# Edges in couples of quads, with the gather's wait moved from the sums to the addition

## The reference, cut to what matters

```
h   = maximum(layernorm(x), 0)
e   = concatenate([h[src], h[dst]], axis=1)        # 200000 x 128
m   = relu(e @ W1 + b1) @ W2 + b2                  # hidden width 128, out 64
s   = segment_sum(m, dst);  cnt = segment_sum(1, dst)
out = x + s / maximum(cnt, 1)
```

## Time and profile before

| | |
|---|---|
| median of 3 runs | 2347.13 us (2336.28 to 2356.41) |
| profiled execution | 2347.96 us, its span 2346.0 us |
| mean granted clock of TensorE | 0.771 |
| busy, share of the span | PE 1445.9 us (62%), PEld 1207.9 (51%), DVE 923.2 (39%), ACT 352.7 (15%), POOL 1480.6 (63%) |
| DMA | 136.93 MB, mean 58 GB/s; the gathers' queue 17.1% of 16 engines' time |

### The profile page before, as it was taken

The page is one execution under the profiler, slowest core; times in us unless marked ns, Lnnn a source line. Parts: engine busy times, 40 slices in busy tenths (PEclk is TensorE's granted clock), DMA queues, the critical chain, the costliest instruction groups (busy, mean ns, idle before and its releaser), DMA issues.

```text
span 2346.0 us, 23165 instructions
## 1 busy us (share of the span) xinstructions
PE 1445.9 (62%) x8389; PEld 1207.9 (51%) x8390; DVE 923.2 (39%) x2278; ACT 352.7 (15%) x704; POOL 1480.6 (63%) x1572
## 2 busy tenths in 40 slices
PE   4451566666666666565666665666665656667667
PEld 3330555555555555554555554555554544555545
DVE  7240334343433343343433433443443433443434
ACT  3230111111111111111111111111111111111111
POOL 5647566666666666666666666666666666665664
PEclk8775777777777777777777778787878877887778
DMA  7532111111111111221212221221221212222221
GB/s 152 148 97 59 43 48 49 50 49 50 48 49 49 50 49 50 51 53 49 62 49 52 52 51 50 61 53 51 53 60 50 52 50 64 55 59 53 65 57 45
DMA packets 107754, 136.93 MB, mean 58 GB/s; under 512 B 30864, under 2 KB 81847, under 8 KB 107635
## 3 DMA queue, kind: packets, MB, share of 16 engines
q0 software_dynamic: 50016, 101.22, 17.1%
q1 hardware_dynamic: 57055, 33.95, 5.4%
q10 hardware_dynamic: 564, 0.23, 0.1%
HBM read 119.21 MB, written 16.07 MB: 58 GB/s over the span
## 4 chain that ended last, share of the span: by engine, by line
another core or an unknown queue 41%; PE 26%; issue 16%; DVE 14%; ACT 2%; DVEq 1%
PE bank L992 8%; PE bank L981 7%; DVE g L759 5%; DVE work L746 4%; PE bank L971 3%; PE bank L1007 2%; DVE work L739 2%; PE bank L999 2%; DVE acc L765 1%; PE bank L871 1%; ACT g L545 1%; PE bank L1017 1%; DVE raw_t L739 1%; DVE stats L612 0%
## 5 line engine op out<-in xcount | busy, mean ns | idle before, releaser
L424 POOL DMA_INDIRECT g<-p_table,src_e x1523 | 1440.9, 946 | 809.6 <-issue 422.6
L992 PE MATMUL bank<-work,g 128*128 128x128 f32 x3126 | 572.5, 329 | 119.7 <-issue 118.4
L992 PEld LDWEIGHTS bank<-work,g 128*128 128x128 f32 x3126 | 493.2, 234 | 188.2 <-issue 185.2
L545 ACT ACTIVATE g<-g 128x512 f32<-128x512 f32 x391 | 246.8, 631 | 1283.0 <-DVE g L759 1032.7
L739 DVE TENSOR_SCALAR_CACHE_REDUCE work<-bank,rows_f 128x512 f32<-128x512 f32 (+1 forms) x261 | 195.0, 747 | 482.7 <-remote 315.7
L981 PEld LDWEIGHTS bank<-work 128*128 128x128 f32 x2086 | 350.5, 238 | 23.2 <-issue 7.5
L981 PE MATMUL bank<-work 128*128 128x128 f32 x2086 | 348.9, 321 | 11.6 <-issue 11.6
L971 PE MATMUL bank<-rel_q,ident 128*128 128x512 bf16 x391 | 183.2, 468 | 254.0 <-DVE work L739 151.5
L765 DVE TENSOR_TENSOR acc<-acc,bank 65x128 f32 x199 | 55.9, 281 | 555.6 <-remote 503.1
L1007 PE MATMUL bank<-sums_u,w 128*64 128x128 f32 x398 | 104.1, 351 | 265.6 <-ACT sums_u L550 170.4
L759 DVE TENSOR_TENSOR g<-bank,g 128x512 f32<-128x512 f32 x391 | 267.7, 685 | 0.0
(11 more groups left out here) (93 smaller groups left out, 419.8 us busy)
## 6 DMA issues: line engine op xcount, KB each, us to landing
g<-p_table,src_e POOLq DMA_INDIRECT x1523
work<-q_table SPq DMA_DIRECT2D x199, 64.0 KB
p_table<-g SPq DMA_DIRECT2D x12, 448.0 KB
q_table<-work SPq DMA_DIRECT2D x12, 448.0 KB
out_dram<-xs SPq DMA_DIRECT2D x5, 448.0 KB
xs<-in_x_dram SPq DMA_DIRECT2D x2, 672.0 KB
xs<-in_x_dram SPq DMA_DIRECT2D x1, 784.0 KB
acc<-in_src_dram SPq DMA_DIRECT2D x1, 768.0 KB
```

The costliest lines, as they stand in the source:

```text
L424: nc.gpsimd.indirect_dma_start(out=g[:, slot(n), j * HID:(j + 1) * HID], out_offset=None, in_=p_table, in_offset=bass.IndirectOffsetOnAxis ...
L545: nc.scalar.activation(g[:, slot(n), 0:w], g[:, slot(n), 0:w], ACT.Relu).then_inc(r_done, 1)
L992: last = nc.tensor.matmul(u_bank[i % 2][:, 0:WIN], g[:, slot(n), HID * c:HID * (c + 1)], member[:, n % MEMBERS, c, :], start=n == GROUPS[i ...
```

## The change

The second stage goes over 196 **couples** of two quads. DVE and ACT do one operation of 1024 columns where they did two of 512, and each semaphore counts couples; in the part with one quad per group a couple holds two windows, so its spread is two operations (`PARTS`) and its two groups are one **block** with one copy and one product with W2. The broadcast on PE is gone: SP writes `rel_q` to a DRAM table once and loads four rows at a time, 4 KB each to all 128 partitions (512 KB), into two buffers, and DVE's spread reads them there. The sum of gathered and q rows no longer goes back into the ring but into one of two places of their own (`both`, a couple each); relu and `sum_edges` use it there. So the gather's wait, once per couple, is for `z_done`, DVE's addition, and the ring has 32 slots; `ahead` starts at 32 and falls by two every 24 quads, to 8. Members have two buffers of a couple and stand ahead of the addition in DVE's order. The core of the diff:

```diff
-RING = 36
-AHEAD_LEAST, AHEAD_STEP = 8, 12
+RING, SLOTS = 32, 36
+AHEAD_LEAST, AHEAD_STEP = 8, 24
 WINDOWS = 8
-MEMBERS = 4
-COUNTS = 8
+COUNTS = 16
...
+def couple(m):
+    return range(2 * m, min(2 * m + 2, QUADS))
...
+BLOCKS = []
+for i, quads in enumerate(GROUPS):
+    if quads[0] % 2:
+        BLOCKS[-1].append(i)
+    else:
+        BLOCKS.append([i])
+BLOCK = [k for m in range(COUPLES) for k, groups_k in enumerate(BLOCKS) if GROUP[2 * m] in groups_k]
+BLOCK_END = [GROUPS[groups_k[-1]][-1] // 2 for groups_k in BLOCKS]
+PARTS = [sorted({GROUP[n] for n in couple(m)}) for m in range(COUPLES)]
...
+    rel_table = nc.dram_tensor("rel_table", [QT * 128, QE], BF16).ap()
...
+        rows_of = [rel_q[:, :, :].rearrange("p t e -> p (t e)"), rows_b[:, :]]
+        g = sb("g", [128, SLOTS, 4 * HID])
         slots = g[:, :, :].rearrange("p k c -> p (k c)")
+        both = [slots[:, 512 * (RING + 2 * k):512 * (RING + 2 * k + 2)] for k in range(2)]
...
+        rows_b = sb("rows_b", [128, 4 * QE], BF16)
+        hs = rows_b[0:NP, :].bitcast(F32).rearrange("p (k t f) -> p k t f", k=HS, f=FEAT)
...
+        qw = [(work if k < 4 else w1_flat)[:, HID * (k % 4):HID * (k % 4 + 1)] for k in range(WINDOWS)]
+        member = work[:, 512:2560].rearrange("p (k c w) -> p k c w", k=2, c=8)
+        spreads = [work[:, 2560 + 1024 * k:2560 + 1024 * (k + 1)] for k in range(2)]
...
+        z_all = [ctx.enter_context(nc.psum_tensor(f"z{i}", [128, 1024], F32)) for i in range(2)]
...
+            sp.wait_ge(row_table, QT)
+            sp.dma_start(rel_table.rearrange("(t q) e -> q t e", q=128), rel_q[:, :, :]).then_inc(rel_out, 16)
...
+            def load_rows(j):
+                if j >= 2:
+                    sp.wait_ge(spread_done, parts_to(2 * (j - 1)))
+                sp.dma_start(rows_of[j % 2], rel_table[4 * j:4 * j + 4, :].rearrange("(o q) e -> o (q e)", o=1)
+                             .to_broadcast([128, 4 * QE])).then_inc(rows_there[j % 2], 16)
...
-                if n >= RING:
-                    ahead = max(AHEAD_LEAST, RING - (n - RING) // AHEAD_STEP)
-                    pool.wait_ge(u_psum, n - ahead + 1)
+                if n >= RING and n % 2 == 0:
+                    ahead = max(AHEAD_LEAST, RING - 2 * ((n - RING) // AHEAD_STEP))
+                    pool.wait_ge(z_done, (n - ahead) // 2 + 1)
                 for j in range(chunks_of(n)):
                     nc.gpsimd.indirect_dma_start(
                         out=g[:, slot(n), j * HID:(j + 1) * HID], out_offset=None, in_=p_table,
                         in_offset=bass.IndirectOffsetOnAxis(ap=src_e[:, 4 * n + j:4 * n + j + 1], axis=0))\
-                        .then_inc(gathered[slot(n)], 16)
+                        .then_inc(gathered[slot(n) // 2], 16)
...
-            def relu(n):
-                w = HID * chunks_of(n)
-                act.wait_ge(z_done, n + 1)
-                nc.scalar.activation(g[:, slot(n), 0:w], g[:, slot(n), 0:w], ACT.Relu).then_inc(r_done, 1)
-            def copy_sums(i):
-                act.wait_ge(u_psum, GROUPS[i][-1] + 1)
-                nc.scalar.copy(sums_u[:, i % 2, :], u_bank[i % 2][:, 0:WIN]).then_inc(u_copied, 1)
+            def relu(m):
+                act.wait_ge(z_done, m + 1)
+                rows = both[m % 2][:, 0:HID * chunks_in(m)]
+                nc.scalar.activation(rows, rows, ACT.Relu).then_inc(r_done, 1)
+            def copy_sums(k):
+                w = WIN * len(BLOCKS[k])
+                act.wait_ge(u_psum, BLOCK_END[k] + 1)
+                nc.scalar.copy(sums_u[:, k % 2, 0:w], u_bank[k % 2][:, 0:w]).then_inc(u_copied, 1)
...
-            def spread_of(n):
-                w = 128 * chunks_of(n)
-                dve.wait_ge(row_done, n + 1)
-                nc.vector.tensor_scalar(spreads[n % 3][:, 0:w], row_bank[:, 0:w], rows_f[:, :], 0.0,
-                                        ALU.is_equal, ALU.add, accum_out=count[:, n % COUNTS:n % COUNTS + 1])\
-                    .then_inc(spread_done, 1)
-            def members_of(n):
-                if n >= MEMBERS:
-                    dve.wait_ge(u_psum, n - MEMBERS + 1)
-                nc.vector.tensor_tensor(member[:, n % MEMBERS, :, :],
-                                        columns_p.unsqueeze(1).to_broadcast([128, 4, WIN]),
-                                        rel_e[:, 4 * n:4 * n + 4].unsqueeze(2).to_broadcast([128, 4, WIN]),
+            def spread_of(m):
+                dve.wait_ge(rows_there[m // 2 % 2], 16 * (m // 4 + 1))
+                at = 0
+                for k, i in enumerate(PARTS[m]):
+                    w = 128 * sum(chunks_of(n) for n in couple(m) if GROUP[n] == i)
+                    row = 2 * QE * (m % 2) + at
+                    j = (parts_to(m) + k) % COUNTS
+                    nc.vector.tensor_scalar(spreads[m % 2][:, at:at + w], rows_of[m // 2 % 2][:, row:row + w], rows_f[:, :],
+                                            0.0, ALU.is_equal, ALU.add, accum_out=count[:, j:j + 1]).then_inc(spread_done, 1)
+                    at += w
+            def members_of(m):
+                if m >= 2:
+                    dve.wait_ge(u_psum, m - 1)
+                nc.vector.tensor_tensor(member[:, m % 2, :, :],
+                                        columns_p.unsqueeze(1).to_broadcast([128, 8, WIN]),
+                                        rel_e[:, 8 * m:8 * m + 8].unsqueeze(2).to_broadcast([128, 8, WIN]),
                                         ALU.is_equal)
-            def add_rows(n):
-                w = HID * chunks_of(n)
-                rows_n = g[:, slot(n), 0:w]
-                dve.wait_ge(zq_done, n + 1)
-                if n < RAW:
-                    dve.wait_ge(raw_p_done, n + 1)
+            def add_rows(m):
+                dve.wait_ge(zq_done, m + 1)
+                if 2 * m < RAW:
+                    dve.wait_ge(raw_p_done, 2 * m + 2)
                 else:
-                    dve.wait_ge(gathered[slot(n)], rows_landed(n))
-                nc.vector.tensor_tensor(rows_n, z_bank[n % 3][:, 0:w], rows_n, ALU.add).then_inc(z_done, 1)
-            def add_sums(i, at):
-                v = sums[:, bass.ds(at, WIN)]
-                dve.wait_ge(v_psum, i + 1)
-                nc.vector.tensor_tensor(v, v, v_bank, ALU.add).then_inc(v_done, 1)
+                    dve.wait_ge(gathered[slot(2 * m) // 2], rows_landed(m))
+                w = HID * chunks_in(m)
+                nc.vector.tensor_tensor(both[m % 2][:, 0:w], z_all[m % 2][:, 0:w], rows_of_p(m), ALU.add)\
+                    .then_inc(z_done, 1)
+            def add_sums(k, firsts):
+                dve.wait_ge(v_psum, k + 1)
+                for j, i in enumerate(BLOCKS[k]):
+                    if j:
+                        dve.wait_ge(v_done, groups_to(k) + j)
+                    v = sums[:, bass.ds(firsts[GROUPS[i][0] % 8], WIN)]
+                    nc.vector.tensor_tensor(v, v, v_bank[:, WIN * j:WIN * (j + 1)], ALU.add).then_inc(v_done, 1)
...
-                for n in range(QUADS + 4):
-                    if n + 2 < QUADS:
-                        spread_of(n + 2)
-                    if n < QUADS:
-                        add_rows(n)
-                    if n + 1 < QUADS:
-                        if n - 1 in MEAN_AT:
-                            dve.wait_ge(o_psum, MEAN_AT.index(n - 1) + 1)
-                        members_of(n + 1)
-                    if 2 <= n < QUADS + 2:
-                        if (n - 2) % 8 == 0:
-                            firsts = first_nodes(dve, n - 2)
-                        i = GROUP[n - 2]
-                        if n - 2 == GROUPS[i][-1]:
-                            add_sums(i, firsts[GROUPS[i][0] % 8])
+                for m in range(COUPLES + 4):
+                    if m + 1 < COUPLES:
+                        spread_of(m + 1)
+                    if m < COUPLES:
+                        if m - 1 in MEAN_AT:
+                            dve.wait_ge(o_psum, MEAN_AT.index(m - 1) + 1)
+                        members_of(m)
+                        add_rows(m)
+                    if 2 <= m < COUPLES + 2:
+                        if (m - 2) % 4 == 0:
+                            firsts = first_nodes(dve, 2 * (m - 2))
+                        k = BLOCK[m - 2]
+                        if m - 2 == BLOCK_END[k]:
+                            add_sums(k, firsts)
...
-            def broadcast_rows(n):
-                w = 128 * chunks_of(n)
-                if n:
-                    pe.wait_ge(spread_done, n)
-                nc.tensor.matmul(row_bank[:, 0:w], ident16[:, n % 128:n % 128 + 1].to_broadcast([128, 128]),
-                                 rel_q[:, n // 128, 0:w], start=True, stop=True).then_inc(row_done, 1)
-            def spread_q(n):
-                pe.wait_ge(spread_done, n + 1)
-                i = GROUP[n]
-                if n == GROUPS[i][0]:
-                    pe.wait_ge(window_in[i % WINDOWS], 16 * (i // WINDOWS + 1))
-                for c in range(chunks_of(n)):
```

(77 more changed lines are left out.)

125 lines of the change are left out of this document (67 added, 58 removed).

## The result

The changed kernel takes 2539.35 us in the median (2532.87 to 2568.08), the kernel before 2344.88 beside it. The ratio is 1.084 (95% interval 1.081 to 1.088): 8.4% slower. Slower was the forecast, by 2%; the time lies outside the range, 89 us above its upper end. Of all the runs reported here one, of the kernel with half of DVE's columns, was in a slower state of the chip; the ratio leaves it out.

The account below looks back on a forecast made before the run. POOL's gather pauses, waiting for PE's late signals, were taken to bound the kernel. 2347.96 us + 52 for longer pauses + 0 for the rest = 2400, less 0.8 to the median: 2399 us; range over the cases 2250 to 2450.

Parts of the forecast that it names:

- the gather's wait, the step that decides: At POOL's gather: pause grows by 2.48 us of members and addition to 4.57, bounds 1.24 and 3.75; +52 us in all.
- What bounds the kernel: POOL's pauses at the gather, for PE's signals held up while POOL gathers: 2.09 us per 2.4 quads, 0.87 a quad.
- The round: Quads between two POOL pauses: two couples or three, 4 or 6 quads, taken as 4.5 in the mean.
- What is given back: The pipe works promptly during the longer pause: prompt stretch 9.1 instead of 6.6 us, 3.6 to 4.0 quads at its pace.
- DVE's operations, PE's relief: DVE: addition and members 1.24 us, spread 1.27, worth nothing; PE: a tenth fewer records, prompt pace 2.5 instead of 2.77 us.
- SP and DMA: 98 row loads of 512 KB cost nothing, covered by two couples; otherwise up to a few us each.
- The rows' place in SBUF: Spread reading SBUF beside POOL's gathers: nothing; bound 0.23 us for each of 196 spreads, 45 us.
- The ring: 32 places stop POOL earlier but the pipe starts some 20 us earlier too: nothing, 6 us either way.
- fewer records win: At the gather: members made before signals fail, only the addition remains, pause 3.33 us; 2301 or 2234 us, chance 0.34.
- it cancels: At the gather: 4.57 us pauses at 4.9 to 5.7 quads a round, within 23 us, 2325 to 2371; chance 0.20.
- POOL pays for the spreads: Gathers beside spreads: the spread's accumulator form holds POOL, 45 us on top, 2444; chance 0.06.
- the gate doesn't matter: At the gather: PE's recovery alone ends pauses, the addition always ready; 100 to 145 us less, 2200 to 2250; chance 0.05.

Follow-up runs that it names:

- the thirteen kernels in the table: The kernel before, the changed kernel and their follow-up variants, each with its ratio, waits and pause per quad; ratios from 0.992 to 1.110.
- couples with the old wait: The changed kernel, but its gather waits for PE's sums of the couple (`u_psum`) instead of DVE's addition: 2334.72 us, ratio 0.996.
- the twins by quads: The kernel before with four places for the sums and a ring of 32: gather waiting for DVE's addition 2494.99 us, for PE's sums 2371.88 us.
- the wait for the relu: The changed kernel, its gather waiting for ACT's relu of the couple (`r_done`) instead of DVE's addition: 2629.67 us, ratio 1.110.
- the rows alone: The kernel before, by quads, with rows brought by SP's 512 KB loads and PE's broadcast removed: 2353.92 us, ratio 0.992.
- signals per quad: The changed kernel with its gather waiting for PE's sums, `u_psum` raised and awaited per quad instead of per couple: 2386.78 us, ratio 1.008.

## Why the prediction was wrong

The mechanism and the direction were right; the step that failed is "the gather's wait, the step that decides", by the size of its term: the pause grew by 6.29 - 2.09 = 4.20 us and not by 2.48.

- *What bounds the kernel.* Held. The pauses make the difference between before and after, and the ratios of the thirteen kernels in the table follow its last column, within the first sets and within the later ones. One reading was too neat: not all of PE's signals wait until POOL is silent, as the sums addition of the earlier trace rows began at 1022.65, beside POOL's last gather.
- *The term that was mis-sized.* The pause was put at 2.09 + 2.48 = 4.57 us and is 6.29. The couples with the old wait split the missing 1.72: they have 2.86, so 0.77 come with the couples, which I had at nothing, and 6.29 - 2.86 = 3.43 with the moved wait, which I had at 2.48. The trace of the changed kernel has both parts in its 79 pauses: from the end of POOL's last gather to the first operation that DVE starts after it 3.2 us in the mean, and from there to POOL's next gather 3.5. DVE began with the members in 46 of them, and in 43 of these POOL followed 2.6 us later: there the 2.48 was right. In 27 it began with the sums addition, 3.8 us after POOL's end in the mean; POOL followed 4.0 us later in 16 of these, and 4.1 to 11.5 in the rest, with means or a further wait in between. That the sums addition waits on PE as well, and stands ahead of spread and members, was in the code and in the earlier trace rows (L765 was the first to start); the bound from above, 3.75, lacked its 0.28, and 2.48 was taken instead of it. At the measured round this is 1.72 / 4.54 x 357 = 135 us, nearly all of the 140 between forecast and result.
- *The round.* 4.5 quads were forecast and 4.54 measured, but that is luck: they came with a pause 1.72 us longer than forecast. With 5.13 us, in the kernel with half of DVE's columns, a round is 4.2 quads; on a line between 2.86 us with 3.4 and 6.29 with 4.54 a pause of 4.57 has about 4.0 (an estimate from these runs). The prediction's own pace gave 3.6 to 4.0, and 4.5 was taken above it; by 4.0 it counted +97 us itself, instead of +52.
- *What is given back.* Nearly what I reasoned at first, one quad in 2.5 us or 0.4 a us: between the twins by quads 1.44 us more of pause gave 0.5 quads, between the couples with the old and the moved wait 3.43 us gave 1.2. Beyond that it is weaker: the wait for the relu gave 0.25 for 1.44 us. After the long pause shown above PE starts slowly: 16 products took 3.56 us at 1036.80 and 1.95 at 1042.86. The windows of PE (stretch, length, busy, granted clock, DMA, GB/s) show the clock of both, near the lower of its two levels (1.2 GHz) after 20.92 us without a matmul, and at the upper (2.4 GHz) a few us later; over the whole span its mean fell from 0.77 to 0.72.

```profile
1036.80:1040.40 3.60, 3.60 (x17) 0.56 0.00 0
1042.80:1044.90 2.10, 2.10 (x20) 1.00 0.66 174
```

- *DVE's operations, PE's relief.* 1.22, 1.21 and 1.27 us measured for 1.24, 1.24 and 1.27. The relief is real and small: the couples with the old wait gain 0.4%, the rows alone 0.8%.
- *SP and DMA* at nothing: held, by the kernel without loads.
- *The rows' place in SBUF* at nothing: held; a gather takes 944 ns, 946 before, and in the changed kernel the 270 gathers that ran beside a spread took 943 ns in the mean, the other 1253 944. So the accumulator form of the spread does not hold POOL. The Trainium skill, "SBUF — State Buffer", in its section "Who interferes with whom", leaves this form out of the operations that can grab the shared port pair, and the trace agrees, 943 beside 944 ns.
- *The ring* at nothing: held; with 32 slots and the old wait the ratio is 1.000.
- *The rivals.* That fewer records win needs the old wait: with it there is 0.4%. That it cancels asked for 4.57 us over 4.9 to 5.7 quads; it was 6.29 over 4.54. That POOL pays for the spreads is refuted by the 943 ns, that the gate doesn't matter by the twins. The direction was a narrow call, 0.41 against 0.39 for faster. Of the signs, pauses for DVE of more than 4 us, fewer than 100 of them, and fewer than 1227 gathers came (6.59 in the mean, 79, 1124); the order members, addition, next gather, expected in each pause, came in 43 of the 79.

Open is why couples lengthen the pause by 0.77 us even with the old wait; signals per quad did not undo it. Open too is why DVE's first operation after POOL's last gather came 2.0 us after it in the kernel before, 2.3 in the couples with the old wait and 3.2 in the changed kernel.

## What to carry to other kernels

Let a producer that must be paused be released by a report of work that is already finished (an old buffer's last reader), not by work that starts only when the report arrives: the first costs the signal's delay, the second the delay and the whole chain behind it. When an in-order engine waits for several late signals, count from the oldest of them, through everything that stands between it and the releasing instruction, a whole turn of the loop if need be; moving an instruction within the loop only changes where the turn begins. An event that comes earlier in the pipe's order is not an earlier release.

## What the runs showed of the hardware

- Without the gathers (POOL sets the slots to zero instead) the same program takes 1270 us instead of 2347, with TensorE's granted clock at 0.94 instead of 0.77 of full speed in the mean. While POOL gathers, PE's signals arrive 8 to 9 us late, 23 us in the changed kernel's pause above, and promptly again some 2 to 3 us after it stops (2.0 us in the mean before, 3.2 in the changed kernel).
- Nothing that was changed on PE, DVE, SP or the ring made the pauses shorter than before: those that end with a report of finished work took 2.1 to 2.3 us beyond 0.30 by quads and 2.9 by couples.
- 96 loads of 512 KB, each spread to 128 partitions beside the gathers, cost no measurable time: 1.087 without them, 1.084 with them.
